# Register loads as steps of their own, memsets between indirect transfers, and another written order

## The reference

```
x = x + 0.5 * quantized_linear(layernorm(x))
x = x + recurrent_block(layernorm(x))               # with its own gelu FFN
x = x + 0.5 * quantized_linear(layernorm(x))
x = x + 0.5 * moe(layernorm(x))                     # pass 0
x = x + gated_linear_attention(layernorm(x))
x = x + 0.5 * moe(layernorm(x))                     # pass 1

def moe(x):                                         # x: (8, 256, 128)
    out = expert(x, Wg_s, Wu_s, Wd_s)               # the shared expert
    probs = sigmoid(x @ Wr.T + rb)                  # 8 experts
    scores, idx = top_k(probs, 2)
    cw = (one_hot(idx, 8) * scores[..., None]).sum(-2)
    for e in range(8):
        out = out + cw[..., e:e + 1] * expert(x, Wg[e], Wu[e], Wd[e])
    return out

def expert(x, Wg, Wu, Wd):                          # inner size 256
    return silu(x @ Wg.T) * (x @ Wu.T) @ Wd.T
```

## Time and profile before

| | us |
|---|---|
| median of 3 runs | 685.3 |
| lowest and highest | 683.61, 685.45 |
| the profiled execution, its span | 692.3 |
| PE busy in the span | 600.1 |
| DVE busy | 497.2 |
| POOL busy | 419.3 |

### The profile page before, as it was taken

How to read it: one execution, slowest core, us unless ns; L and a number is a source line. 1 busy time by engine, 2 the same in 40 slices (tenths; PEclk the granted TensorE clock), 3 DMA queues, 4 the chain that set the end, 5 groups by cost and what they waited for, 6 DMA issues and landing times.

```text
span 692.3 us, 14370 instructions
## 1 busy us (share of the span) xinstructions
PE 600.1 (87%) x4124; PEld 476.3 (69%) x4124; DVE 497.2 (72%) x1721; ACT 387.7 (56%) x1019; POOL 419.3 (61%) x445
## 2 busy tenths in 40 slices
PE   0366999999989998999897899999999999978974
PEld 0224565655666797888696686769879989857863
DVE  7997999978998865557224798989877766553335
ACT  2395968988766545444353728466565355533541
POOL 5276696488567777567643614553776575775552
PEclk9996999999999999999999999999999999999997
DMA  7999000001033355666768600124216556566796
GB/s 258 410 411 371 0 1 1 1 0 32 13 99 94 97 156 161 186 193 180 211 176 245 235 6 1 35 66 131 74 43 172 153 151 177 161 182 189 231 297 232
DMA packets 60125, 100.97 MB, mean 146 GB/s; under 512 B 10288, under 2 KB 28592, under 8 KB 59792
## 3 DMA queue, kind: packets, MB, share of 16 engines
q1 hardware_dynamic: 50832, 81.52, 38.5%
q0 software_dynamic: 8640, 17.84, 7.4%
q10 hardware_dynamic: 576, 0.69, 0.3%
HBM read 61.79 MB, written 38.23 MB: 144 GB/s over the span
## 4 chain that ended last, share of the span: by engine, by line
PE 43%; DVE 13%; DMA 9%; issue 6%; POOL 3%; SPq 2%; ACT 2%; POOLq 0%; DVEq 0%; ACTq 0%
PE bank L1083 13%; PE bank L1058 6%; PE bank L1296 5%; DMA tin<-rows_by_expert 3%; PE bank L969 3%; PE bank L955 3%; PE bank L944 2%; DMA hid<-rows_done 2%; DMA rows_done<-tout,tdst 2%; PE bank L1064 2%; DMA rows_done<-tout,tin 1%; POOL rows_by_expert L840 1%; DVE qt L417 1%; PE bank L312 1%; PE bank L307 1%
## 5 line engine op out<-in xcount | busy, mean ns | idle before, releaser
L840 POOL DMA_INDIRECT rows_by_expert<-xx,sidx x128 | 128.1, 1001 | 72.2 <-issue 34.0
L1083 PE MATMUL bank<-tint,twt 128*128 128x128 f32 x1136 | 151.8, 282 | 6.0 <-DVE thidt L1121 3.4
L1083 PEld LDWEIGHTS bank<-tint,twt 128*128 128x128 f32 x1136 | 141.1, 196 | 22.0 <-issue 12.3
L1132 POOL DMA_INDIRECT rows_done<-tout,tin x98 | 96.3, 983 | 57.5 <-ACT tout L1107 34.8
L1121 DVE TENSOR_TENSOR thidt<-tsil,bank 128x256 f32<-128x256 f32 x142 | 58.2, 418 | 95.8 <-ACT tsil L1099 74.1
L1099 ACT ACTIVATE tsil<-bank 128x256 f32<-128x256 f32 x142 | 53.9, 384 | 89.9 <-PE bank L1083 88.4
L1058 PE MATMUL bank<-e_dn,thidt 128*128 x568 | 90.6, 286 | 15.5 <-DVE thidt L1121 7.3
L1058 PEld LDWEIGHTS bank<-e_dn,thidt 128*128 128x128 f32 x568 | 76.8, 195 | 25.2 <-issue 24.8
L1107 ACT ACTIVATE tout<-bank,tin 128x128 f32<-128x128 f32 x142 | 50.2, 366 | 62.9 <-PE bank L1064 43.7
L1132 POOL DMA_INDIRECT rows_done<-tout,tdst x44 | 43.7, 993 | 49.0 <-ACT tout L1107 35.9
L1296 PEld LDWEIGHTS bank<-bufA,bufB 128*127 128x127 f32 (+6 forms) x448 | 47.7, 176 | 11.6 <-issue 6.7
(11 more groups left out here) (272 smaller groups left out, 1331.0 us busy)
## 6 DMA issues: line engine op xcount, KB each, us to landing
twt<-moe_gu SPq DMA_DIRECT2D x142, 256.0 KB
rows_by_expert<-tout SPq DMA_DIRECT2D x25, 715.0 KB, 20.0
tin<-rows_by_expert SPq DMA_DIRECT2D x142, 65.0 KB, 2.6
hid<-rows_done SPq DMA_DIRECT2D x12, 512.0 KB, 5.5
x<-x_in SPq DMA_DIRECT2D x8, 256.0 KB, 4.4
rows_by_expert<-xx,sidx POOLq DMA_INDIRECT x128
out<-x SPq DMA_DIRECT2D x8, 256.0 KB, 3.9
rows_done<-tout,tin POOLq DMA_INDIRECT x98
```

Source lines behind the costliest of these rows:

```text
L840: pool.indirect_dma_start(out=rows_by_expert, out_offset=bass.IndirectOffsetOnAxis(ap=sidx[h][:, k:k + 1], axis=0), in_=xx[h][:, r, t, :], ...
L1083: m = pe.matmul(bank[UP_BANKS[p][j]][:, c * P:(c + 1) * P], weights[:, c * P:(c + 1) * P], tint[g % TURNS][:, :], start=True, stop=True)
L1132: pool.indirect_dma_start(out=rows_done, out_offset=bass.IndirectOffsetOnAxis(ap=dst, axis=0), in_=tout[:, g % RING, :], in_offset=None).t ...
```

## The change

Four things are changed.

1. PE's register loads are calls of their own, `x_ids_tensor`, with a wait for the table alone. There are 38 as before. Each has its own place in PE's order, ahead of the step that uses the registers.
2. `r_scatter_gpsimd` issues one indirect transfer in a call instead of two, so a unit has eight calls, and others can stand between any two of them.
3. Between two indirect transfers that followed each other directly on POOL stands a memset of 128 partitions by 112 fp32 numbers to a tile that nothing reads (`t_pause_gpsimd`). The written order has 253 of them (the words of the change say 249). Each waits for the memset four earlier.
4. The order on all five engines is another.

```
+PAUSES, PAUSE = 4, 112
...
+        pause = sb("pause", [P, PAUSES, PAUSE])
...
+        s_pause = sem("s_pause")
...
         def r_scatter_gpsimd(pool, u, p, q):
...
-            for k in (2 * q, 2 * q + 1):
-                r, t = k // TILES, k % TILES
-                pool.indirect_dma_start(out=rows_by_expert, out_offset=bass.IndirectOffsetOnAxis(
-                    ap=sidx[h][:, k:k + 1], axis=0), in_=xx[h][:, r, t, :], in_offset=None).then_inc(s_scat[h], 16)
+            r, t = q // TILES, q % TILES
+            pool.indirect_dma_start(out=rows_by_expert, out_offset=bass.IndirectOffsetOnAxis(
+                ap=sidx[h][:, q:q + 1], axis=0), in_=xx[h][:, r, t, :], in_offset=None).then_inc(s_scat[h], 16)
...
+        def x_ids_tensor(pe, p, j):
+            pe.wait_ge(s_table, WAVES * p + wave_of(j) + 1)
+            expert_pe.update(values_of(ENG.PE, etab[p], chunk_at(j), E_ROUTED))
...
         def x_io_tensor(pe, p, s):
...
-                if chunk_at(j):
-                    pe.wait_ge(s_table, WAVES * p + wave_of(j) + 1)
-                    expert_pe.update(values_of(ENG.PE, etab[p], chunk_at(j), E_ROUTED))
                 pe.wait_ge(s_thid, g + 1)
...
+        def t_pause_gpsimd(pool, i):
+            if i >= PAUSES:
+                pool.wait_ge(s_pause, i - PAUSES + 1)
+            pool.memset(pause[:, i % PAUSES, :], 0.0).then_inc(s_pause, 1)
...
+            t_pause_gpsimd(pool, 0)
+            r_scatter_gpsimd(pool, 0, 0, 1)
```

More of the change, by code:

```diff
@@ L1536, in _ @@
                 t_weights_sync(sp_, 0, j)
-            for j in range(35, 39):
+            for j in range(36, 39):
                 t_load_sync(sp_, 0, j)
@@ L2079, in _ @@
             g_value_vector(dve, 1)
+            x_dst_vector(dve, 0, 67)
             g_first_vector(dve, 1)
             g_level_vector(dve, 0, 0)
+            for j in range(68, 70):
+                x_dst_vector(dve, 0, j)
             g_level_vector(dve, 1, 0)
@@ L2096, in _ @@
             g_level_vector(dve, 1, 6)
-            x_hid_vector(dve, 0, 70)
-            g_stats_vector(dve, 4)
+            for j in range(69, 71):
+                x_hid_vector(dve, 0, j)
+            c_add_vector(dve, 5, 0)
             g_add_vector(dve, 0)
@@ L2741, in _ @@
-            q_mul_tensor(pe, 7, 1)
-            x_io_tensor(pe, 0, 13)
-            for j in range(9, 12):
+            q_mul_tensor(pe, 6, 1)
+            e_down_tensor(pe, 3, 0)
+            x_up_tensor(pe, 0, 7)
+            for j in range(10, 12):
+                x_io_tensor(pe, 0, j)
+            r_turn_tensor(pe, 5, 0)
+            x_up_tensor(pe, 0, 8)
+            q_turn_tensor(pe, 7, 1)
+            q_mul_tensor(pe, 7, 1)
+            for j in range(9, 11):
+                x_up_tensor(pe, 0, j)
@@ L2762, in _ @@
-            e_gate_tensor(pe, 5, 0, 0)
+            x_ids_tensor(pe, 0, 21)
+            r_turn_tensor(pe, 6, 0)
+            x_io_tensor(pe, 0, 18)
+            for j in range(15, 19):
+                x_up_tensor(pe, 0, j)
+            e_down_tensor(pe, 4, 0)
             for j in range(19, 21):
@@ L2913, in _ @@
             g_turn_tensor(pe, 2)
-            x_io_tensor(pe, 0, 75)
+            for j in range(74, 76):
+                x_io_tensor(pe, 0, j)
             g_turn_tensor(pe, 3)
@@ L3182, in _ @@
                 x_io_tensor(pe, 1, j)
-            for j in range(59, 62):
+            for j in range(59, 61):
                 x_up_tensor(pe, 1, j)
@@ new lines, in _ @@
+            x_out_scalar(act, 0, 5)
+            q_copy_scalar(act, 7, 1)
+            x_in_scalar(act, 0, 11)
+            x_silu_scalar(act, 0, 8)
+            x_out_scalar(act, 0, 6)
+            for j in range(9, 11):
+                x_silu_scalar(act, 0, j)
+            e_silu_scalar(act, 4, 0, 0)
+            x_out_scalar(act, 0, 7)
+            for j in range(12, 15):
+                x_in_scalar(act, 0, j)
+            x_silu_scalar(act, 0, 11)
+            r_xt_scalar(act, 5, 0)
+            x_out_scalar(act, 0, 8)
@@ new lines, in _ @@
+            for j in range(36, 38):
+                x_out_scalar(act, 0, j)
+            for j in range(39, 41):
+                x_silu_scalar(act, 0, j)
+            e_silu_scalar(act, 7, 0, 0)
+            for j in range(43, 45):
+                x_in_scalar(act, 0, j)
+            x_out_scalar(act, 0, 38)
+            for j in range(41, 45):
+                x_silu_scalar(act, 0, j)
+            x_in_scalar(act, 0, 45)
+            e_silu_scalar(act, 7, 0, 1)
+            for j in range(39, 42):
+                x_out_scalar(act, 0, j)
@@ new lines, in _ @@
+            for j in range(46, 48):
+                x_in_scalar(act, 0, j)
+            for j in range(42, 44):
+                x_out_scalar(act, 0, j)
+            x_in_scalar(act, 0, 48)
+            for j in range(45, 47):
+                x_silu_scalar(act, 0, j)
+            x_in_scalar(act, 0, 49)
+            x_out_scalar(act, 0, 44)
+            for j in range(47, 49):
+                x_silu_scalar(act, 0, j)
+            x_out_scalar(act, 0, 45)
+            x_in_scalar(act, 0, 50)
@@ L3551, in _ @@
+            for j in range(46, 48):
+                x_out_scalar(act, 0, j)
+            for j in range(51, 53):
+                x_in_scalar(act, 0, j)
+            for j in range(49, 51):
                 x_silu_scalar(act, 0, j)
@@ L3743, in _ @@
+            x_in_scalar(act, 1, 16)
+            x_silu_scalar(act, 1, 15)
+            x_out_scalar(act, 1, 11)
+            r_tanh_scalar(act, 5, 1)
+            for j in range(12, 14):
+                x_out_scalar(act, 1, j)
+            x_silu_scalar(act, 1, 16)
+            x_in_scalar(act, 1, 17)
+            x_silu_scalar(act, 1, 17)
+            for j in range(18, 20):
+                x_in_scalar(act, 1, j)
+            x_silu_scalar(act, 1, 18)
+            for j in range(14, 16):
                 x_out_scalar(act, 1, j)
-            x_silu_scalar(act, 1, 14)
+            e_silu_scalar(act, 5, 1, 0)
@@ L3775, in _ @@
+            g_late_scalar(act, 6, 6)
+            for j in range(23, 25):
+                x_in_scalar(act, 1, j)
             for j in range(18, 20):
@@ L3881, in _ @@
+            for j in range(52, 54):
                 x_silu_scalar(act, 1, j)
```

2436 lines of the change are left out of this document (1399 added, 1037 removed).

## The result

| | us |
|---|---|
| before, median of 4 runs | 684.45 (680.82 to 685.45) |
| changed, median of 4 runs | 698.72 (695.00 to 700.99) |
| ratio | 1.021, 95% interval 1.017 to 1.025 |
| span of the profiled execution | 692.3 before, 696.6 changed |

14 us slower, where 1.5 us faster was forecast; the range ended at 692. The spans differ by 4.3 us only. In every run with both on record the time is 1.8 to 1.9 us more than the span, so the profiled execution of before took some 694.1 us (an estimate: 692.3 + 1.8), 9.7 us above the median of 684.45. The changed kernel's profiled execution took 698.43 us and lies at its median.

A forecast was written before the change was run, and what follows sets the result against it. PE was taken as the bound where nearly always busy, DVE in the first 50 us. Terms -3.8 + 1.9 + 1.4 - 1.0 = -1.5 us on 692.3 gave 690.8, scaled by 0.990 to 683.8 us; range 675.5 to 692.

The forecast's parts named there:

- What bounds the kernel: Whole kernel: where PE is nearly always busy, only its own work or losses matter; DVE paces the first 50 us.
- The rival on DVE beside POOL: From 400 to 500 us: memsets hold DVE up to 0.19 us each, 8.6 us; some 688 to 692 us; chance 0.04.
- The memsets: POOL between transfers: 0.19 us more per pair, 48 us on POOL; 1.9 us lost on PE (0 to 7).
- The last wave of pass 1: Unit 7's eight scatters: landing 8 x 0.19 = 1.5 us later, PE waiting; taken as +1.4 us (0 to 3.9).
- The loads: PE's register loads as own calls: gains of 4.3 and 1.5 us, 2.0 lost; sum -3.8 us (-9 to 0).
- the seven large gaps: PE idle at seven register loads, 6.6 us together, shrinking to the typical gap: 4.3 us gained.
- the other 31 loads: PE's remaining register loads: said to lose 0.09 to 0.44 us each, 5.8 us together.
- The four pairs: Four places on PE where two loads stand together: the second costs half its time, 4 x 0.5 = 2.0 us lost.
- The end: Last tiles: additions behind all products remove PE waits of 1.50 and 3.01 us; taken as -1.0 us (-5 to +4).
- The base: Starting point of the sum: the profiled execution's 692.3 us, with the result scaled by 0.990 to the runs' median.

The follow-up runs named there:

- short POOL operations: POOL's four two-input operations of 128x512 cut to 128x8, in both kernels: changed 676.42 us (0.986 of before), before 669.49 us (0.976).

## Why the prediction was wrong, point by point

- **What bounds the kernel.** That nothing but PE's own work or losses can change a stretch in which PE is full was the step that failed. From 400 to 500 us PE was at 96.31 only because DVE, at 90.78 of 100, just kept up. The row showed an engine with 9 us to spare on which PE's products in the scan depend, and the new order of that stretch was costed at nothing. It cost 7.8 us by the traces, 6.4 of which go with short POOL operations. The new order in the experts of pass 0 was costed at nothing as well, beyond loads and memsets; see the last point.
- **The rival on DVE beside POOL.** It had the right rows and the wrong culprit. I asked whether the memsets hold DVE, and they don't (under 2 us over some 300 operations). I did not ask which of POOL's old operations the new order moves beside which of DVE's. Two additions of units in a row make one hold of some 2.5 us beyond the operation's own length where before single ones cost 1 us (a pair held an operation in before too, at 390.83 us, where PE did not wait for it). The 28 us against 14 of such time were to be looked for in the order, at L1202. And one reason given against the rival was wrong: from 400 to 500 us only 63 of DVE's 312 operations read PSUM, 34 of its 90.78 us; 117 are the scan's products, all with inputs in SBUF alone. That its 688 to 692 us had a mechanism near the true one is luck, since it held the memsets to be the cause.
- **The memsets.** Length right (0.21 for 0.19), gaps wrong: the memset sits in a good part of the 0.30 us. 0.08 us for 0.19, 20 us of POOL for 48. POOL's idle time from 291 to 341 us shrank from 12.9 to 6.1 us as said. PE's waits for rows fell by 2.8 us instead of costing 1.9; the traces show up to 3 us of delay in pass 0 all the same, given back later.
- **The last wave of pass 1.** 1.4 us predicted. The lag on the trace of before is 7.0 us at the 3600th matmul and 8.0 at the 3840th: 1.0 us. The size is right by luck. The eight scatters take 9.4 us from the first start to the last for 9.05 before, 0.3 us more and not 1.5, and PE doesn't wait for rows at all there, where 3.3 us was to be seen. It waits 4.20 us at 620.02 for DVE, which is busy with the wave's routing and table, and gets most of that back.
- **The loads.** -3.8 us predicted, -5.5 measured within the new order (the comparison has no interval of its own). At the seven large gaps the prediction was right, 6.6 us. Of the other 31 loads only 12 have a gap, 0.09 to 0.44 us, 2.4 us together and not 5.8. All gaps at loads went from 9.0 to 4.8 us. The four pairs lose 2.1 us, for 2.0 predicted; two gaps of 0.81 and 0.84 us stand behind other products, and one of 0.69 us behind a transpose, where none over 0.5 was to be left.
- **The end.** -1.0 us predicted. The lag falls from 8.0 us at the 3840th matmul to 4.5 at the end of the span, -3.5. The mechanism is in the rows: the last tile's down product ends at 679.7 us in both traces of the table, so PE has won all 8.0 us by then, and 4.5 of them are paid back behind it.
- **The base.** The sum was made against an execution taken to be 7 us above the median, which was 9.7 above it, and then scaled by 0.990. That assumed that the excess lay evenly. Between the matmuls 960 and 1920 before's trace takes 8.1 us longer than its version with short operations, the changed kernel's only 3.2 us, so the excess probably lies in the experts of pass 0 and hid a loss of the new order there. No trace of before from an execution of 683 us was had, so this is read, not shown.
- **What stays open.** With short operations the lag grows by 2.9 us from matmul 840 to 1920, in the experts of pass 0, and by 1.8 to 2160, in small waits for `thidt`, silu and issue; no experiment took this apart. If all of before's excess lies in pass 0, the 14 us are, as an estimate from the table of matmuls: under 1 us up to the 840th, some 8 from there to the 2160th, 7.8 in the linear attention and the experts beside it, and 2.5 won back behind the 3600th. Only the 6.4 us of the third term have a cause shown by an experiment.

## What to carry to other kernels

When an order is rewritten, list for the second engine what stands beside it now, and not just who waits for whom: here a DVE operation of 0.42 us with two SBUF inputs took 3.2 us beside two GpSimd additions back to back. A stretch with one engine at 96% and its partner at 91% has two bounds; two holds of 2.8 and 3.0 us on the partner came out as 5.0 us of waits. The partner's busy time alone doesn't tell it: in the first 200 us the same kind of hold cost nothing at the end. And before a sum is built on one profiled execution, its time should be near the median; some 10 us of unexplained excess are more than any term of this sum.

## What the runs showed of the hardware

- A transfer issued by GpSimd takes 0.96 us and 0.30 us pass before the next; a memset of 0.21 us between them makes the step 1.34 instead of 1.26 us.
- DVE's operation at 497.62 us handles 8 columns and took 3.14 us beside two GpSimd additions of 1.25 us each, though it started 0.6 us before them; the same operation took 0.16 us at 496.87 us, so it should have been done by then.
- All runs of a series on one chip can be disturbed (801 us) and those of another on the same chip not (683 us). Up to the 800th matmul, some 200 us in, the traces of both are within 3.3 us of each other.
